# Attention scores by pairs of heads in one pass, with keys and queries laid out through HBM

## The chip, the cores and the metric

The kernel runs on one core of a Trainium2 chip, as one launch. The metric is the device time of that launch in microseconds (us).

## What is computed

The input x is (16, 96, 16, 16). The reference, cut to its parts:

```
x = conv_lstm(x)        # row by row recurrence over 16 rows, 48 features; skip conv; x + skip
t = tokens(x)           # (16, 256, 96): 256 tokens of 96 channels for each of 16 samples
q, k, v = six heads of 16 from layernorm(t)
scores = einsum('bhtd,bhsd->bhts', q, k) * 96 ** -0.5 ; causal mask ; softmax
t = t + (scores @ v, heads joined) @ Wp + bp
t = t + ffn(layernorm(t))   # 4 experts of 384 hidden, top 2 of 4, gelu
```

The weight and projection matmuls before the softmax and the router are done with operands split into a high and a low part (fp32r), so that three products make one of near float32 accuracy.

## The kernel before, in words

The kernel is written with one program for each engine, and semaphores between them. It has two stages. First comes the recurrence, which ends at about 81 us of the span. Then a loop over NBLK = 8 blocks of BT = 512 tokens, that is two samples (a = 0, 1) of two tiles (t = 0, 1) of 128 tokens. The first and the last block are written out, the rest is a loop.

Within a block the attention is done in NU = 10 units, listed in UNITS. A unit is some heads of one tile: for t = 0 (128 keys) HG[0] = 3 heads, so 384 columns of scores; for t = 1 (256 keys) HG[1] = 2 heads, so 512 columns. So units 0, 1 and 5, 6 have 384 columns, units 2 to 4 and 7 to 9 have 512. Scores go into one of two PSUM banks S[u % 2], probabilities into one of three slots of p_sb.

For each unit: TensorE makes the scores (L942 to L966) and adds the causal mask with a bf16 matmul (L965); VectorE takes the negated row maximum (L704); ScalarE the exponentials, an instruction per head, with their sum (L518); VectorE the reciprocal (L710); POOL scales the rows, an instruction per head (L406); TensorE transposes them (L976); VectorE or ScalarE copies the transposes (L457, which of them by PT_ON_ACT); TensorE multiplies with the values (L997). After the last unit of a tile ScalarE copies the heads' output (L527) and TensorE projects it (L1003), and VectorE makes the residual and its statistics (L717 to L721), from which POOL makes the reciprocal deviation (L389, L391).

The order on TensorE is written out by hand in its body (L1040). In step j it makes the scores of unit j + 2, then FILL[j] pieces of the expert output of the block before (L1018), then the values of unit j - 1, then the transposes of unit j. After the last step come the next block's queries and keys (L853 to L855), the transposes of the second layer norm (L1089), the hidden layer of the experts in 12 chunks of three matmuls (L1034, L1035, L1038), with the router between them. The scores of the next block's unit 0 stand after the ninth chunk (L1106), those of unit 1 after the last chunk and the values' projection (L1111). Block 0 has no expert output of a block before.

**Keys and queries.** ScalarE and VectorE split the projected queries into q_cur (high, low) and the keys into k_cur (high, low), 96 rows of 6 heads x 16 (L498, L691, L502, L696). Six heads are used as two triples. q_st holds for each triple 48 rows of high parts and 48 rows of low parts. k_bd holds block-diagonal keys: for each head of the triple its own columns, in pass 0 the high part against both halves of the query rows, in pass 1 the low part against the high queries. The rest of k_bd is zero, from a memset at the start (L375). So each group of scores takes two matmuls (L960, L962). The copies run on DMA from one place of SBUF to another, issued by SP (SyncE): per block 4 for the queries (load_queries, L289) and 24 for the keys (load_keys, L318: for each sample, triple and head one of 32 KB and one of 16 KB). In block 0 the query copies are issued by POOL (L441 to L443). SP's order in a block (body, L334): wait for the last scores of the block before, queries, wait for the low keys, keys of the first sample, store the output of an earlier block (L332), keys of the second sample, stage the tokens of a later block (L316). A wait that must stand alone on its instruction is made by wait_alone (L271).

TensorE waits for the queries and for the keys of the sample and triple that a unit needs (L945 to L953). At a block's end ScalarE waits for all the copies before it overwrites q_cur and k_cur (L551 to L555).

Of the kernel before, what the change touches and what calls it, by code (L numbers as in the profile page):

```python
# [20 lines left out]
F32 = mybir.dt.float32  # L21
# [13 lines left out]
HEADS, HS = 6, 16  # L35
# [14 lines left out]
HG = (3, 2)  # L50
UNITS = [(a, t, h) for a in range(2) for t in range(2) for h in range(0, HEADS, HG[t])]
NU = len(UNITS)
TILE_END = [1 + max(u for u, (a, t, _) in enumerate(UNITS) if 2 * a + t == s) for s in range(SPB)]
# [8 lines left out]
def hybrid_kernel(nc, x, w_input, w_state, b_skip, wq, wk, wv, wp, bp,  # L62
                  gate_w, gate_b, w1, b1, w2, b2, ident, ident_bf, causal_bf, lower, out):
    with ExitStack() as ctx:
# [183 lines left out]
        q_in = [sem("q_in0"), sem("q_in1")]  # L248
        q_in_first = [sem("q_in_first0"), sem("q_in_first1")]
        kbd_in = [[sem(f"kbd_in{a}{g}") for g in range(2)] for a in range(2)]  # L250
# [13 lines left out]
        KBD = 6 * 16  # L264
        TRI = 3 * HS
# [16 lines left out]
        def queries_taken(eng, n, g):  # L282

            if isinstance(n, int) and n == 0:
                eng.wait_ge(q_in_first[g], 32)
            else:
                eng.wait_ge(q_in[g], 32 * n)

        def load_queries(eng, g, taken):  # L289

            for part in range(2):
                eng.dma_start(as_f32(q_st[part * TRI:(part + 1) * TRI, g, :]),
                              as_f32(q_cur[g * TRI:(g + 1) * TRI, part, :])).then_inc(taken[g], 16)


        @block.sync
        def _(sp):
# [20 lines left out]
            def load_keys(a, g):  # L318

                cols = slice(a * 2 * TT, (a + 1) * 2 * TT)  # L320
                for i in range(3):
                    h = 3 * g + i
                    rows_h = slice(h * HS, (h + 1) * HS)
                    upper, lower_ = slice(i * HS, (i + 1) * HS), slice(TRI + i * HS, TRI + (i + 1) * HS)
                    sp.dma_start(as_f32(k_bd[upper, a, :, g, i, :]), as_f32(k_cur[rows_h, :, cols])
                                 ).then_inc(kbd_in[a][g], 16)
                    sp.dma_start(as_f32(k_bd[lower_, a, 0, g, i, :]), as_f32(k_cur[rows_h, 0, cols])
                                 ).then_inc(kbd_in[a][g], 16)
# [5 lines left out]
            def body(n, first=False, store=True, more=True):  # L334
                if first:
                    sp.wait_ge(klo_done, 1)
                    load_keys(0, 0)
                    load_keys(0, 1)
                else:
# [32 lines left out]
        def _(pool):  # L372
# [26 lines left out]
            def scale(n, u):  # L399

                wait_alone(pool, rden_done, NU * n + u + 1)
                _, t, _ = UNITS[u]
                nk = TT * (t + 1)
                for i in range(HG[t]):
# [44 lines left out]
        def take_pt(eng, n, u, first=False):  # L449

            t = UNITS[u][1]
            w = HG[t] * (t + 1) * TT
# [8 lines left out]
        def _(act):  # L461
# [48 lines left out]
            def exps(n, u, first=False):  # L510
# [4 lines left out]
                _, t, _ = UNITS[u]  # L515
                nk = TT * (t + 1)
                for i in range(HG[t]):
# [11 lines left out]
            def body(n, first=False, last=False):  # L529
# [19 lines left out]
                if not last:  # L549

                    for per_sample in kbd_in:  # L551
                        for taken in per_sample:
                            act.wait_ge(taken, KBD * (n + 1))
                    for g in range(2):
                        queries_taken(act, n, g)  # L555
                    take_q(n + 1)
                    take_k(n + 1)
# [28 lines left out]
        def _(dve):  # L586
# [112 lines left out]
            def row_max(n, u):  # L699

                _, t, _ = UNITS[u]
                nk = TT * (t + 1)
                dve.wait_ge(scores_ready, NU * n + u + 1)
                V.tensor_reduce(nmax[:, u % 3, 0:HG[t]], S[u % 2][:, 0:HG[t] * nk].rearrange("p (h k) -> p h k", k=nk),  # L704
                                AX.X, ALU.max, negate=True).then_inc(max_done, 1)

            def recip(n, u):
                dve.wait_ge(exp_done, NU * n + u + 1)
                hg = HG[UNITS[u][1]]
# [138 lines left out]
        def _(pe):  # L848
# [93 lines left out]
            def scores(n, u):  # L942
                a, t, h0 = UNITS[u]
                nh, nk, s = HG[t], TT * (t + 1), 2 * a + t
                if u >= 2:  # L945
                    pe.wait_ge(exp_done, NU * n + u - 1)
                elif u == 0:
                    pe.wait_ge(qlo_done, n + 1)
                    pe.wait_ge(klo_done, n + 1)
                if u < 2:  # L950
                    queries_taken(pe, n, u)
                if t == 0:
                    pe.wait_ge(kbd_in[a][h0 // 3], KBD * (n + 1))  # L953
# [249 lines left out]
```

## Time and profile before

| what | us |
|---|---|
| median of 3 runs | 471.73 (471.09 to 473.12) |
| span of the profiled execution, first to last instruction | 469.8 |
| recurrence | about 81 |
| TensorE busy | 429.3 (91%) |
| VectorE busy | 269.8 (57%) |
| ScalarE busy | 263.7 (56%) |
| POOL busy | 146.5 (31%) |

The profile shows one execution. Its own time is given as its span; the median of the runs is 1.9 us above it. Busy TensorE matmuls overlap each other, so that the mean duration of one is longer than what it adds to the time; the chain of work that ended last, read in order of time, gives what each adds. "Idle before, releaser" tells how long an engine waited and for what. PEld is TensorE's load of the stationary operand, beside the matmuls. SPq is SP's queue of DMA issues. The granted clock of TensorE is 1.00 at 2.4 GHz and 0.50 at 1.2 GHz.

### The profile page before, as it was taken

Reading aid. Unit: us, or ns where it says so; the run is one execution under the profiler, and the core shown is the slowest. Engines: PE = TensorE matmul, PEld = TensorE weight load, DVE = VectorE, ACT = ScalarE, POOL = GpSimd, SP = SyncE. Lnnn points to the kernel's source line nnn. Section 1 sums busy time; section 2 is a strip of 40 time slices with the busy share of each in tenths; the row PEclk is TensorE's granted clock in tenths of the full one; section 3 lists DMA queues with packets and bytes.
Section 4 is the critical chain, followed back from the end, with each engine's and each line's share of the span. In section 5 each row is a group of like instructions: output and inputs, shape, how many; then the busy total and the mean of one; then the engine's idle time right before and its main releaser. Section 6 shows DMA issues by size and latency. Waiting matters only on the chain.

```text
span 469.8 us, 10623 instructions
## 1 busy us (share of the span) xinstructions
PE 429.3 (91%) x3112; PEld 344.1 (73%) x3112; DVE 269.8 (57%) x954; ACT 263.7 (56%) x740; POOL 146.5 (31%) x309
## 2 busy tenths in 40 slices
PE   6999995449779999999999999999999999999897
PEld 6989994325558767877787787778767877787676
DVE  3888887445523853585277527743763586267424
ACT  2444453236557556664866485568556664866370
POOL 5000000235521542254236215531543254235200
PEclk9999998557979999999999999999999999999999
DMA  8500000031021002100210121012002100210000
GB/s 201 130 0 0 0 0 0 17 71 32 3 57 29 19 0 59 44 17 14 66 38 0 38 51 28 0 46 52 19 0 54 46 0 4 76 22 3 7 11 17
DMA packets 14392, 14.93 MB, mean 32 GB/s; under 512 B 5426, under 2 KB 11412, under 8 KB 14372
## 3 DMA queue, kind: packets, MB, share of 16 engines
q1 hardware_dynamic: 14180, 14.30, 12.1%
q0 software_dynamic: 192, 0.39, 0.3%
q8 instruction: 9, 0.15, 0.1%
q14 instruction: 11, 0.09, 0.1%
HBM read 3.86 MB, written 1.57 MB: 12 GB/s over the span
## 4 chain that ended last, share of the span: by engine, by line
PE 73%; DVE 12%; ACT 5%; issue 5%; SPq 2%; DMA 1%; POOL 1%; DVEq 1%; ACTq 0%; POOLq 0%
PE F L1018 18%; PE T L976 9%; PE A L997 8%; PE F L1034 4%; PE F L1038 4%; PE S L960 4%; PE F L1035 4%; PE S L962 3%; PE F L1014 3%; PE S L965 2%; DVE c L629 2%; DVE ig L627 2%; ACT tc_sb L471 2%; DVE pt_sb L457 1%; PE M L939 1%
## 5 line engine op out<-in xcount | busy, mean ns | idle before, releaser
L406 POOL TENSOR_SCALAR p_sb<-p_sb,rden 128x128 f32<-128x128 f32 (+1 forms) x192 | 79.8, 431 | 135.0 <-DVE rden L710 132.8
L1018 PE MATMUL F<-w_sb,hid 128*128 128x96 f32 x768 | 101.0, 276 | 0.0
L1018 PEld LDWEIGHTS F<-w_sb,hid 128*128 128x128 f32 x768 | 93.4, 192 | 6.0 <-issue 6.0
L518 ACT ACTIVATE p_sb<-S,nmax 128x128 f32<-128x128 f32 (+1 forms) x192 | 78.9, 425 | 17.1 <-DVE nmax L704 17.0
L704 DVE TENSOR_REDUCE nmax<-S 128x2 f32<-128x512 f32 (+1 forms) x80 | 50.7, 634 | 52.7 <-PE S L965 52.3
L457 ACT COPY pt_sb<-T 128x512 f32<-128x512 f32 (+1 forms) x48 | 26.4, 550 | 68.7 <-PE T L976 68.7
L564 ACT ACTIVATE hid<-F,b_sb 128x512 f32<-128x512 f32 x72 | 49.3, 686 | 9.6 <-PE F L1038 9.0
L997 PE MATMUL A<-pt_sb,v_cur 128*32 128x128 f32 x576 | 44.2, 284 | 8.5 <-ACT pt_sb L457 4.5
L976 PE MATMUL T<-id_sb,p_sb 128*128 128x128 f32 x288 | 49.2, 290 | 1.5 <-POOL p_sb L406 1.4
L960 PE MATMUL S<-k_bd,q_st 96*128 96x384 f32 (+2 forms) x96 | 39.3, 416 | 6.5 <-DMA k_bd<-k_cur 6.4
L976 PEld LDWEIGHTS T<-id_sb,p_sb 128*128 128x128 f32 x288 | 30.9, 143 | 16.3 <-issue 13.9
L518 ACT ACTIVATION_READ_ACCUMULATOR p_sb<-S,nmax 128x1 f32 x192 | 39.9, 208 | 0.0
L997 PEld LDWEIGHTS A<-pt_sb,v_cur 128*32 128x32 f32 x576 | 22.3, 109 | 20.4 <-ACT pt_sb L457 9.5
L962 PE MATMUL S<-k_bd,q_st 96*128 96x384 f32 (+2 forms) x96 | 32.9, 349 | 0.0
L779 DVE SCALAR_TENSOR_TENSOR y_sb<-F,gw,y_sb 128x96 f32<-128x96 f32 x96 | 30.5, 318 | 3.4
L1034 PE MATMUL F<-x2hi,w1hi 96*128 96x512 f32 x72 | 30.6, 425 | 1.4 <-ACT x2hi L559 0.8
L865 PE MATMUL F<-x_pad,win_sb 96*112 (+1 forms) x192 | 27.2, 291 | 4.5 <-DMA x_pad<-in_x 4.5
L457 DVE COPY pt_sb<-T 128x384 f32<-128x384 f32 (+1 forms) x32 | 20.0, 624 | 18.4 <-PE T L976 18.4
L1038 PE MATMUL F<-x2lo,w1hi 96*128 96x512 f32 x72 | 29.7, 413 | 0.0
L471 ACT ACTIVATE tc_sb<-c 48x128 f32<-48x128 f32 x32 | 9.9, 309 | 35.2 <-DVE c L629 35.2
L1035 PE MATMUL F<-x2hi,w1lo 96*128 96x512 f32 x72 | 28.9, 401 | 0.0
L865 PEld LDWEIGHTS F<-x_pad,win_sb 96*112 96x112 f32 x192 | 24.9, 193 | 4.4 <-DVE win_sb L596 4.4
(140 smaller groups left out, 781.8 us busy)
## 6 DMA issues: line engine op xcount, KB each, us to landing
k_bd<-k_cur SPq DMA_DIRECT2D x96, 32.0 KB, 2.0
q_st<-q_cur SPq DMA_DIRECT2D x28, 96.0 KB, 2.2
k_bd<-k_cur SPq DMA_DIRECT2D x96, 16.0 KB, 1.8
t_st<-t_cm SPq DMA_DIRECT2D x7, 192.0 KB, 2.4
out_y<-y_sb SPq DMA_DIRECT2D x7, 192.0 KB, 1.9
x_pad<-in_x SPq DMA_DIRECT2D x2, 612.0 KB, 8.6
w_sb<-in_w SPq DMA_DIRECT2D x1, 576.0 KB
hid<-in_w SPq DMA_DIRECT2D x1, 576.0 KB, 6.9
```

Source lines behind the costliest of these rows:

```text
L406: last = nc.gpsimd.tensor_scalar(p, p, rden[:, u % 3, i:i + 1], 1.0, ALU.mult, ALU.mult)
L457: copy(pt_sb[:, u % 2, 0:w], T[:, 0:w]).then_inc(pt_done, 1)
L518: last = nc.scalar.activation(p_sb[:, u % 3, i * nk:(i + 1) * nk], S[u % 2][:, i * nk:(i + 1) * nk], ACT.Exp, bias=nmax[:, u % 3, i:i + 1] ...
L564: nc.scalar.activation(hid[:, c, :], L1[c % 4][:], ACT.Gelu, bias=b1_sb[:, c:c + 1]).then_inc(gelu_done, 1)
L704: V.tensor_reduce(nmax[:, u % 3, 0:HG[t]], S[u % 2][:, 0:HG[t] * nk].rearrange("p (h k) -> p h k", k=nk), AX.X, ALU.max, negate=True).then ...
L865: last = mm(G[q][0:GATE_M, c * HC:(c + 1) * HC], wi_sb[:, tap, c], xr[:, bs, tap:tap + W], start=(c == 0 and tap == 0), stop=ready, skip_g ...
L960: mm(d, q_st[:, g, ts], k_bd[:, a, 0, g, i0:i1, 0:nk], start=(3 * g + i0 == h0), stop=False, skip_group_check=True)
L976: last = nc.tensor.transpose(T[:, i * TT:(i + 1) * TT], p_sb[:, u % 3, i * TT:(i + 1) * TT], id_sb[:])
L997: last = mm(A[VW * (h % 3):VW * (h % 3) + VW, 0:TT], v, pt_sb[:, u % 2, c0:c0 + TT], start=(kt == 0 and h < 3), stop=(kt == t and h >= 3), ...
L1018: last = mm(dst[:, e * C:(e + 1) * C], hid[:, c, s * TT:(s + 1) * TT], w2_sb[:, c], start=False, stop=(c == NCH - 1), skip_group_check=True)
L1034: mm(dst, w1hi[:, cs], x2hi[:], start=True, stop=False)
L1038: mm(dst, w1hi[:, cs], x2lo[:], start=False, stop=True).then_inc(hid_ready, 1)
```

## The change

For t = 0 a unit is now 4 heads and then 2, in place of 3 and 3; for t = 1 it stays at 2. Heads are used in three pairs. q_st holds for each pair 96 rows: 32 rows of high, 32 of low, 32 of high parts. k_bd holds for each pair 96 rows, the high keys, the high keys and the low keys, block-diagonal for the two heads and for all 512 tokens. One matmul makes the scores of a pair.

The layout is made in HBM. Per block SP issues: q_cur stored to q_hbm (1), the key parts high, high, low stored to their places in k_hbm (3), then, once each has landed, the query rows loaded (3, one for each 32 rows of q_st) and the keys loaded (3, one for each pair): 10 in place of 28. k_hbm is laid out so that a store of 6 heads x 16 rows puts each head's rows into its own columns; its zeros are stored once, at the start, from the zeroed k_bd (2 transfers). In all blocks these transfers are SP's. Before the query store SP waits for the key and query loads of the block before. TensorE waits for all query rows and for a pair's keys, ScalarE as before for all.

The diff, cut to its core (the rest hands the number of heads nh of a unit through the helpers):

```diff
-HG = (3, 2)
-UNITS = [(a, t, h) for a in range(2) for t in range(2) for h in range(0, HEADS, HG[t])]
+HG = (4, 2)
+NPAIR = HEADS // 2
+PAIR = 2 * HS
+UNITS = [(a, t, h, min(HG[t], HEADS - h)) for a in range(2) for t in range(2) for h in range(0, HEADS, HG[t])]
...
-        q_st = sb("q_st", [C, 2, BT], F32R)
+        q_st = sb("q_st", [C, NPAIR, BT], F32R)
...
-        k_bd = sb("k_bd", [C, 2, 2, 2, 3, 2 * TT], F32R)
+        k_bd = sb("k_bd", [C, NPAIR, 2, BT], F32R)
+        q_hbm = nc.dram_tensor("q_hbm", [C, 2, BT], F32, kind="Internal").ap()
+        k_hbm = nc.dram_tensor("k_hbm", [2 * PAIR * NPAIR * 2 * BT + HEADS * (HS * NPAIR * 2 + 1) * BT], F32, kind="Internal").ap()
...
+        QIN, KBD = 3 * 16, 16
+        Q_PARTS, K_PARTS = (0, 1, 0), (0, 0, 1)
...
+        def pair_taken(eng, n, g):
+
+            eng.wait_ge(q_in, QIN * (n + 1))
+            eng.wait_ge(kbd_in[g], KBD * (n + 1))
...
+            KROW = NPAIR * 2 * BT
+            KHEAD = HS * KROW + BT
+            KROWS = C + (NPAIR - 1) * PAIR
+            k_rows = k_hbm[0:KROWS * KROW].rearrange("(p c) -> p c", c=KROW)
+
+            def send_queries():
+
+                sp.dma_start(q_hbm[:], as_f32(q_cur[:])).then_inc(q_out, 16)
+
+            def send_keys():
+
+                for j, part in enumerate(K_PARTS):
+                    at = j * PAIR * KROW
+                    dst = k_hbm[at:at + HEADS * KHEAD].rearrange("(h s) -> h s", h=HEADS)
+                    dst = dst[:, 0:HS * KROW].rearrange("h (r c) -> h r c", r=HS)[:, :, 0:BT]
+                    sp.dma_start(dst, as_f32(k_cur[:, part, :])).then_inc(kbd_out, 16)
+
+            def fetch_queries(n):
+
+                wait_alone(sp, q_out, 16 * n + 16)
+                for j, part in enumerate(Q_PARTS):
+                    sp.dma_start(as_f32(q_st[j * PAIR:(j + 1) * PAIR]),
+                                 q_hbm.rearrange("(g r) p t -> p r g t", g=NPAIR)[part]).then_inc(q_in, 16)
+
+            def fetch_keys(n):
+
+                wait_alone(sp, kbd_out, 3 * 16 * (n + 1))
+                for g in range(NPAIR):
+                    sp.dma_start(as_f32(k_bd[:, g].rearrange("p x t -> p (x t)")),
+                                 k_rows[g * PAIR:g * PAIR + C, g * 2 * BT:(g + 1) * 2 * BT]).then_inc(kbd_in[g], 16)
...
             def body(n, first=False, store=True, more=True):
-                if first:
-                    sp.wait_ge(klo_done, 1)
-                    load_keys(0, 0)
-                    load_keys(0, 1)
-                else:
+                wait_alone(sp, qlo_done, n + 1)
+                if not first:
+                    for g in range(NPAIR):
+                        wait_alone(sp, kbd_in[g], KBD * n)
+                    wait_alone(sp, q_in, QIN * n)
+                send_queries()
+                wait_alone(sp, klo_done, n + 1)
+                send_keys()
+                if not first:
                     wait_alone(sp, scores_ready, NU * n)
-                    wait_alone(sp, qlo_done, n + 1)
-                    load_queries(sp, 0, q_in)
-                    load_queries(sp, 1, q_in)
-                    wait_alone(sp, klo_done, n + 1)
-                    load_keys(0, 0)
-                    load_keys(0, 1)
+                fetch_queries(n)
+                fetch_keys(n)
                 if store:
                     store_y(n - 2)
-                load_keys(1, 0)
-                load_keys(1, 1)
                 if more:
                     wait_alone(sp, tt_ready, n + 2)
                     stage(n + 2)
 
             sp.wait_ge(zeroed, 5)
+            for r0, r1 in ((0, C), (C, KROWS)):
+                sp.dma_start(k_rows[r0:r1], as_f32(k_bd[0:r1 - r0].rearrange("p g x t -> p (g x t)"))
+                             ).then_inc(kbd_zero, 16)
+            sp.wait_ge(kbd_zero, 32)
...
-            pool.wait_ge(qlo_done, 1)
-            load_queries(nc.gpsimd, 0, q_in_first)
-            load_queries(nc.gpsimd, 1, q_in_first)
...
-                for g in range(h0 // 3, (h0 + nh - 1) // 3 + 1):
-                    i0, i1 = max(h0 - 3 * g, 0), min(h0 + nh - 3 * g, 3)
-                    d = dst[:, 3 * g + i0 - h0:3 * g + i1 - h0]
-
-                    mm(d, q_st[:, g, ts], k_bd[:, a, 0, g, i0:i1, 0:nk], start=(3 * g + i0 == h0), stop=False,
-                       skip_group_check=True)
-                    mm(d, q_st[:, g, ts], k_bd[:, a, 1, g, i0:i1, 0:nk], start=False, stop=False,
+                ks = slice(a * 2 * TT, a * 2 * TT + nk)
+                for i in range(0, nh, 2):
+                    g = (h0 + i) // 2
+                    if a == 0 and t == 0:
+                        pair_taken(pe, n, g)
+                    mm(dst[:, i:i + 2], q_st[:, g, ts], k_bd[:, g, :, ks], start=(i == 0), stop=False,
                        skip_group_check=True)
```

## Rows read from the trace of the kernel before

**Rows 1.** The page: span, and part 1, busy time of each engine.

```profile
span 469.8 us, 10623 instructions
PE 429.3 (91%) x3112; PEld 344.1 (73%) x3112; DVE 269.8 (57%) x954; ACT 263.7 (56%) x740; POOL 146.5 (31%) x309
```

**Rows 2.** The page, part 4: the chain that ended last, by engine.

```profile
PE 73%; DVE 12%; ACT 5%; issue 5%; SPq 2%; DMA 1%; POOL 1%; DVEq 1%; ACTq 0%; POOLq 0%
```

**Rows 3.** Windows, one period of the loop: busy us (instructions), clock, DMA share, GB/s.

```profile
191.44:235.66 44.22, 43.20 (x320) 33.95 (x320) 25.15 (x87) 28.21 (x81) 17.16 (x37) 1.00 0.12 32
```

**Rows 4.** The chain in order of time, three units' scores: start us, us, what.

```profile
238.51 0.26 PE S L960
238.77 0.23 PE S L962
239.00 0.13 PE S L965
...
240.88 0.12 PE S L960
...
241.36 0.12 PE S L965
...
247.77 0.20 PE S L960
247.98 0.17 PE S L962
248.15 0.18 PE S L965
```

**Rows 5.** Groups by line and form: busy us, mean ns | idle before.

```profile
L406 POOL TENSOR_SCALAR p_sb<-p_sb,rden 128x128 f32<-128x128 f32 x96 | 34.8, 380 | 97.6 <-DVE rden L710 96.8
L518 ACT ACTIVATE p_sb<-S,nmax 128x128 f32<-128x128 f32 x96 | 34.3, 376 | 7.8 <-DVE nmax L704 7.8
```

**Rows 6.** Timeline of POOL and TensorE around unit 5: start us, us.

```profile
251.24 1.10 POOL L406 TENSOR_SCALAR p_sb<-p_sb,rden 128x128 f32<-128x128 f32 x3
...
252.84 0.55 PE L976 MATMUL T<-id_sb,p_sb 128*128 128x128 f32 x3
```

**Rows 7.** Timeline of four engines, from a block's keys to the next block's scores.

```profile
265.28 2.42 SPq L292 DMA_DIRECT2D q_st<-q_cur  x4
...
265.96 0.68 DVE L696 TENSOR_TENSOR k_cur<-S,k_cur 96x512 fp32r<-96x512 f32 x1
...
267.88 0.66 SPq L325 DMA_DIRECT2D k_bd<-k_cur  x1
...
275.30 0.34 PE L960 MATMUL S<-k_bd,q_st 96*128 96x384 f32 x1
```

**Rows 8.** DMA issues: count, KB each, median us from issue to landing.

```profile
out_y<-y_sb SPq DMA_DIRECT2D x7, 192.0 KB, 1.9
...
win_sb<-in_w_input SPq DMA_DIRECT2D x1, 252.0 KB, 3.0
```

**Rows 9.** The page, part 3: queue, packets, MB, share of 16 engines' span.

```profile
q1 hardware_dynamic: 14180, 14.30, 12.1%
```

**Rows 10.** DMA of 462 to 470 (the last stores), and GB/s in 40 slices of 187 to 191.

```profile
q1 hardware_dynamic: 288, 0.20, 7.7%
...
GB/s 0 0 0 0 92 113 92 31 0 0 61 82 21 0 0 0 108 353 338 399 353 307 108 0 0 82 102 103 41 0 0 41 92 31 0 0 0 0 72 113
```

**Rows 11.** Timeline of VectorE and TensorE at the first block's scores.

```profile
93.34 0.69 DVE L691 SCALAR_TENSOR_TENSOR q_cur<-S,q_cur 96x512 fp32r<-96x512 f32 x1 [0.60 <-ACT q_cur L498]
...
99.20 0.66 PE L960 MATMUL S<-k_bd,q_st 96*128 96x384 f32 x1 [4.87 <-DMA k_bd<-k_cur]
...
102.02 0.66 PE L960 MATMUL S<-k_bd,q_st 96*128 96x384 f32 x1 [1.50 <-DMA k_bd<-k_cur]
```

**Rows 12.** Windows around block 0's end; the column after POOL is the granted clock.

```profile
126.00:131.00 5.00, 2.50 (x18) 1.44 (x16) 2.18 (x7) 2.01 (x4) 1.72 (x5) 0.99 0.00 0
131.00:135.00 4.00, 3.24 (x9) 2.37 (x10) 1.19 (x2) 2.40 (x3) 2.03 (x2) 0.50 0.41 111
135.00:137.00 2.00, 2.00 (x6) 1.53 (x5) 0.00 (x0) 0.84 (x2) 0.00 (x0) 0.50 0.19 41
```

More of the change, by code:

```diff
@@ L47 @@
 GATE_STEPS = 14
-HG = (3, 2)
-UNITS = [(a, t, h) for a in range(2) for t in range(2) for h in range(0, HEADS, HG[t])]
+HG = (4, 2)
+NPAIR = HEADS // 2
+PAIR = 2 * HS
+UNITS = [(a, t, h, min(HG[t], HEADS - h)) for a in range(2) for t in range(2) for h in range(0, HEADS, HG[t])]
 NU = len(UNITS)
-TILE_END = [1 + max(u for u, (a, t, _) in enumerate(UNITS) if 2 * a + t == s) for s in range(SPB)]
+TILE_END = [1 + max(u for u, (a, t, _, _) in enumerate(UNITS) if 2 * a + t == s) for s in range(SPB)]
 FILL = [16, 3, 3, 2, 3, 3, 2, 2, 2, 0]
@@ L247, in hybrid_kernel @@
         t_staged = sem("t_staged")
-        q_in = [sem("q_in0"), sem("q_in1")]
-        q_in_first = [sem("q_in_first0"), sem("q_in_first1")]
-        kbd_in = [[sem(f"kbd_in{a}{g}") for g in range(2)] for a in range(2)]
+        q_in = sem("q_in")
+        q_out = sem("q_out")
+        kbd_out = sem("kbd_out")
+        kbd_zero = sem("kbd_zero")
+        kbd_in = [sem(f"kbd_in{g}") for g in range(NPAIR)]
         y_out = sem("y_out")
@@ L280, in as_f32 @@
             return ap.bitcast(F32)
-        def queries_taken(eng, n, g):
-            if isinstance(n, int) and n == 0:
-                eng.wait_ge(q_in_first[g], 32)
-            else:
[L287 to L293, printed above, removed]
+        def pair_taken(eng, n, g):
+            eng.wait_ge(q_in, QIN * (n + 1))
+            eng.wait_ge(kbd_in[g], KBD * (n + 1))
         @block.sync
@@ L316, in stage @@
                 sp.dma_start(t_st[:], t_cm[:, bass.ds(n * BT, BT)]).then_inc(t_staged, 16)
[L318 to L328, printed above, removed]
+            KROW = NPAIR * 2 * BT
[20 more added lines that the diff above has]
+                                 k_rows[g * PAIR:g * PAIR + C, g * 2 * BT:(g + 1) * 2 * BT]).then_inc(kbd_in[g], 16)
             def store_y(n):
@@ L401, in scale @@
                 wait_alone(pool, rden_done, NU * n + u + 1)
-                _, t, _ = UNITS[u]
+                _, t, _, nh = UNITS[u]
                 nk = TT * (t + 1)
-                for i in range(HG[t]):
+                for i in range(nh):
                     p = p_sb[:, u % 3, i * nk:(i + 1) * nk]
@@ L449, in take_pt @@
         def take_pt(eng, n, u, first=False):
-            t = UNITS[u][1]
-            w = HG[t] * (t + 1) * TT
+            _, t, _, nh = UNITS[u]
+            w = nh * (t + 1) * TT
             eng.wait_ge(pt_ready, NU * n + u + 1)
@@ L514, in exps @@
                     act.wait_ge(pt_ready, NU * n + u - 2)
-                _, t, _ = UNITS[u]
+                _, t, _, nh = UNITS[u]
                 nk = TT * (t + 1)
-                for i in range(HG[t]):
+                for i in range(nh):
                     last = nc.scalar.activation(p_sb[:, u % 3, i * nk:(i + 1) * nk], S[u % 2][:, i * nk:(i + 1) * nk],
@@ L549, in body @@
                 if not last:
[L551 to L555, printed above, removed]
+                    for g in range(NPAIR):
+                        pair_taken(act, n, g)
                     take_q(n + 1)
@@ L973, in probs_t @@
                     pe.wait_ge(x2lo_done, n)
-                t = UNITS[u][1]
-                for i in range(HG[t] * (t + 1)):
+                _, t, _, nh = UNITS[u]
+                for i in range(nh * (t + 1)):
                     last = nc.tensor.transpose(T[:, i * TT:(i + 1) * TT], p_sb[:, u % 3, i * TT:(i + 1) * TT], id_sb[:])
@@ L979, in values @@
             def values(n, u, first=False):
-                a, t, h0 = UNITS[u]
+                a, t, h0, nh = UNITS[u]
                 s = 2 * a + t
@@ L991, in values @@
                 for kt in range(t + 1):
-                    for i in range(HG[t]):
+                    for i in range(nh):
                         h = h0 + i
```

20 lines of the change are left out of this document (5 added, 15 removed).

## The prediction

> **What bounds the kernel now.** The page comes first: TensorE is busy in 91% of the span and makes 73% of the chain that ended last [rows 1, 2]. Then one period of the loop over blocks by windows: 44.22 us, of which TensorE is busy 43.20 [rows 3]. The six whole periods look alike. So an instruction taken off TensorE counts, as long as nothing else then ends TensorE's wait. The profiled execution spans 469.8 us, 1.9 below the median of 471.7; the sum is made against the span and 1.9 is added.
>
> **Part 1: fewer score passes.** Before, a unit multiplies each triple of heads twice, by the high and by the low part of the keys; after, each pair once, with the same 96 rows (q high, q low, q high against k high, k high, k low). The group view gives 416 and 349 ns for these matmuls, but they overlap; what one adds is read from the chain in order of time. A unit with 512 columns costs 0.26 + 0.23 and 0.13 for the mask; 256 columns cost 0.12; a unit with 384 costs 0.20 + 0.17 and 0.18 for the mask [rows 4]. A block has four units of 384 and six of 512, which the chain puts at 5.82 us in all. After, six units of 512 take one pass and the mask (0.39 each), two units of four heads take two passes of 256 and a mask of 512 (about 0.50), two of two heads one pass of 256 and a mask of 256 (about 0.27): 3.88. So 1.94 us a block, 15.5 in eight. The number of transposes, value matmuls, exponentials and reductions per block stays, and so do their widths in sum.
>
> **Part 2: units of 3 + 3 heads become 4 + 2.** Columns in sum are the same, but the first unit of each pair is longer. POOL takes 0.36 us per further head to scale, ScalarE about 0.35 (start to start; 376 and 380 ns each in the rows) [rows 5]. Before, POOL ends the scaling of unit 5 at 252.34 and its transposes start at 252.84: 0.5 spare [rows 6]. After, POOL ends 0.36 later, while TensorE comes about 0.5 sooner, because the scores of units 6 and 7 between the two have shrunk (0.28 and 0.23). So it waits some 0.3 there, and I take 0.2 more for the same at unit 7, behind the wider copy of unit 5: 0.5 a block given back, 4 in all. Bounds: nothing, and 1.5, if POOL, VectorE and ScalarE set the pace of all middle units.
>
> **Part 3: keys and queries through HBM.** Before, the scores of the next block's unit 0 start at 275.30, 8.66 after VectorE ends k_cur (265.96 + 0.68) [rows 7]. That distance stays: between them lie the x2 transposes, nine hidden chunks and the router, none of them changed. In it 12 SP issues and a landing had to fit; the first leaves at 267.88, 0.18 after the last query transfer, so a wait on SP costs about 0.18 [rows 7]. Now the rows must go out, land, and be fetched.
> SP: the queries are ready at 265.2; four new waits (three on keys, one on queries, all long met) put the query store at 265.9, the first key store at 266.8, the third at 268.1. The store of 192 KB lands 1.9 after its issue [rows 8]; about 0.8 of this is packets, so the first byte takes some 0.9, the close 0.2.
> How fast a store moves depends on how many DMA engines share it. Every larger transfer of the trace has an outermost dimension of 16, 48, 96, 112 or 128 rows; the new key store is written as 6 heads x 16 rows. One small case bears on it: the queue shows 14,180 packets [rows 9]; the pieces of its 258 transfers, one for each run of bytes in a row, add up to 10,066, which leaves 4,114 closing packets, 14 fewer than 258 x 16. Just the load of b2, with two rows, would be 14 short if it ran on 2 engines. So I take six engines for the key stores. The Trainium skill says this as a rule ("DMA: Bandwidth & Descriptors", why a DMA increments its semaphore by 16): the engines are the largest number up to 16 that divides the outermost dimension of both sides, here 6. By that rule the sum below stands; if a store always had 16 engines, the first rival would.
> One engine moves 20 GB/s in the last stores (0.20 MB in 7.7% of 8 us x 16 engines) and 25 at the best (399 GB/s over 16) [rows 10]. Three stores of 196 KB over six engines are 98 KB each, 3.9 to 4.9 us. They start behind the query store's packets at 268.0 and have landed at 272.1 to 273.1; SP sends the first two key loads at 272.3 to 273.3 and 0.65 later. Their bytes start 0.9 later, and on the six engines only after the query loads queued there (37 KB, 1.5 to 1.9 us: 273.4 to 274.8). Two key loads of 24.6 KB per engine take 2.0 to 2.6. Unit 0 can start at 275.6 to 277.8, where it was due at 275.30: a wait of 0.3 to 2.5; I take 1.5, the middle. As a check on this, a load of 252 KB lands after 3.0 [rows 8]. It falls on six of the seven hand-overs: at the first, block 0 runs at the lower clock and leaves 11.3 us. 6 x 1.5 = 9.0.
> Unit 1 needs pair 2, 0.65 later, and is due 3.4 after unit 0: covered. VectorE's maxima and the gelus shift with TensorE and are not late by themselves.
>
> **Part 4: the start.** Before, unit 0 runs at 99.20 and unit 1 at 102.02, both waiting for keys [rows 11]. Now SP stores the queries at 94.1 (after q_cur ends, 93.34 + 0.69), then the keys; six engines end at 100.4 to 101.3, the first two key loads have landed at 105 to 106, unit 1 follows at 106 to 107. Against 102.02 that is 4 to 5 later, and block 0 has no expert work of the block before to fill the gap: + 4.7. The stores of zeros (2 MB) run while the recurrence does, which ends at 81: nothing. The memset of k_bd halves, hidden too, as are the four query transfers that leave POOL and the 18 issues fewer on SP.
>
> **The sum.** 469.8 - 15.5 + 4.0 + 9.0 + 4.7 = 472.0; with 1.9 it is 473.9, say 474: the matmuls saved are given back in waits.
>
> **Rivals.** Half a percent, 2.4 us, is about what a measurement here can tell from no change.
> *Stores on all engines (faster).* The same bytes over 16 engines: 37 KB each, 1.5 to 1.9. The stores have landed by 270.1, while SP is issuing query loads until 271.1; key loads leave at 271.3 and 272.0 and have landed at 274.5 to 275.1, before 275.30. No wait in the loop, and a start later by 2.5: 469.8 - 15.5 + 4 + 2.5 + 1.9 = 462.7. For it: every large row shows full spread. Against: the count of closing packets. 0.25.
> *Six engines, but short waits.* The best ends of part 3 (0.3 to 0.7 a block): 474 - 6 x 1.0 = 468. 0.12.
> *The attention chain sets the pace (slower).* Its place is the scaling of unit 5 and of units 7 and 8 on POOL, where the spare before is 0.5; from there on each 0.1 that TensorE comes sooner is a wait of 0.1. If 1.5 of the 1.94 go back, it is 474 + 8 = 482. For: VectorE, ScalarE and POOL work through these units nearly without a gap. Against: their work in sum is unchanged, and the early units have more than 1 us spare. 0.15.
> *The clock falls (slower).* After a gap of 2.5 in block 0 the stretch 131 to 135 ran at 0.50, where 126 to 131 had 0.99, and was not back before 137 [rows 12], over 6 us. If a wait of over 2 us at the hand-over did this, some 3.3 more per block: 474 + 20 = 494. Against: before such a wait TensorE would have been busy without a pause, which it was not there. 0.03.
> That the two passes don't become one can't be: the loop issues one matmul per pair.
>
> **How the numbers follow.** Forecast 0.45, with 470 to 478 as its own range. Faster by over 0.5% (below 469.4): the first rival, most of the second, a little of the forecast: 0.34. Slower (above 474.1): the two slow rivals and half of the forecast: 0.39. The rest 0.27. The range goes from a little below the first rival, whose own bounds are as wide, to the third: 460 to 482.
>
> **What would show it.** One group of score matmuls x96 where there were two, a mean between 256 and 512 columns; a period near 44.2. At the hand-over, TensorE's wait for k_bd from k_hbm: 1.5 us, six times; key stores landing 4 to 5 us after the last issue (on 16 engines: 2). A small wait for POOL's p_sb before the transposes of units 5 and 7. Unit 1 of block 0 at 106 to 107. The forecast is wrong if the stores land within 2.5 us, or if the period is under 43.3 or over 45.

## The result, and the profile after

The changed kernel is slower, and by far more than forecast: 549.65 us in the median against 471.09 us for the kernel before in the same comparison, a ratio of 1.152 with a 95% interval of 1.144 to 1.160. The ratio takes only executions within 1.5% of the fastest of their kernel, here those of 540.9 and 545.2 us, so it lies below the quotient of the medians, 1.167. The forecast was 474, the range 460 to 482. The five executions of the changed kernel lie between 540.9 us, at a mean granted clock of 0.88, and 578.5 us, at 0.81: the stretches of low clock described below are not equally long in each. The profiled one took 570.9 us, at 0.82; times inside an execution are from it.

The page after: span, part 1 (busy time of each engine), the clock line of part 2 (granted clock in tenths, in 40 slices of 14.2 us), q1 of part 3, the engines of part 4, and one group of part 5.

```profile
span 569.1 us, 10328 instructions
PE 479.9 (84%) x3001; PEld 385.0 (68%) x3016; DVE 269.7 (47%) x954; ACT 262.8 (46%) x740; POOL 140.8 (25%) x305
PEclk9999975585656995699569955996799689959999
q1 hardware_dynamic: 13620, 30.84, 19.5%
PE 49%; DMA 16%; DVE 15%; issue 6%; ACT 5%; POOL 3%; SPq 3%; another core or an unknown queue 2%; DVEq 1%; POOLq 0%; ACTq 0%
L973 PE MATMUL S<-k_bd,q_st 96*128 96x256 f32 (+1 forms) x96 | 45.9, 492 | 50.0 <-DMA k_bd<-k_hbm 48.6
```

The work did shrink: 3001 matmul records for 3112 [rows 1], one group of score matmuls x96. Yet TensorE is busy 50.6 us longer, which no added work explains, and DMA makes 16% of the chain that ended last, where it made 1% [rows 2]. The clock line is the new thing: before, the digits were low in block 0 only, up to the twelfth slice of 11.7 us, as the page before shows:

```profile
PEclk9999998557979999999999999999999999999999
```

After, it dips in every block. Windows of after: one period of the loop (from one copy of x2hi to the next), then stretches inside it, and two at the start. The columns are those of [rows 3]; the clock is the third number from the end.

```profile
261.26:319.30 58.04, 51.47 (x308) 40.54 (x308) 25.14 (x86) 28.11 (x81) 17.07 (x37) 0.79 0.19 54
262.00:269.50 7.50, 7.50 (x33) 5.68 (x34) 2.26 (x8) 6.42 (x10) 2.71 (x3) 1.00 0.56 163
269.50:275.70 6.20, 1.09 (x4) 0.39 (x3) 0.00 (x0) 1.15 (x2) 0.00 (x0) 0.68 0.79 212
275.70:282.00 6.30, 6.30 (x19) 5.25 (x20) 0.69 (x1) 2.84 (x4) 0.00 (x0) 0.50 0.10 31
282.00:290.00 8.00, 8.00 (x32) 6.49 (x31) 3.19 (x15) 3.20 (x15) 1.42 (x4) 0.50 0.00 0
298.00:319.30 21.30, 19.94 (x173) 15.63 (x171) 15.21 (x53) 11.06 (x41) 11.03 (x26) 1.00 0.03 8
87.50:107.50 20.00, 4.51 (x15) 3.46 (x15) 5.29 (x8) 3.53 (x5) 1.27 (x1) 0.50 0.42 119
128.00:152.00 24.00, 19.24 (x81) 12.86 (x81) 8.09 (x23) 8.99 (x20) 7.83 (x15) 0.51 0.17 44
```

Read them in order. Up to 269.5 TensorE works without a pause at full clock. From 269.5 to 275.7 it is almost idle while the DMA engines are busy. Then it works without a pause again, at a granted clock of 0.50 (1.2 GHz), and only by 298 is it back at 1.00. The records put the fall at 271.8 and the return at 295.6: 23.9 us. VectorE and ScalarE, whose own work per period is unchanged (25.14 and 28.11 for 25.15 and 28.21), only wait for TensorE there.

What the idle stretch waits for stands in the chain of that stretch in order of time (start us, us, what):

```profile
260.52 0.60 DVE k_cur L715
...
261.19 0.79 SPq L337
...
262.80 7.37 DMA k_hbm<-k_cur
...
270.23 0.32 SPq L350
...
270.60 4.90 DMA k_bd<-k_hbm
...
275.63 0.55 PE S L973
```

and in the timelines of SP's queue and of TensorE over the same stretch:

```profile
260.39 0.33 SPq L329 DMA_DIRECT2D q_hbm<-q_cur  x1
261.19 2.28 SPq L337 DMA_DIRECT2D k_hbm<-k_cur  x3
263.89 3.42 SPq L343 DMA_DIRECT2D q_st<-q_hbm  x3
270.23 1.26 SPq L350 DMA_DIRECT2D k_bd<-k_hbm  x3
...
274.05 0.58 PE L973 MATMUL S<-k_bd,q_st 96*128 96x256 f32 x1 [4.11 <-DMA k_bd<-k_hbm]
275.63 0.55 PE L973 MATMUL S<-k_bd,q_st 96*128 96x256 f32 x1 [1.00 <-DMA k_bd<-k_hbm]
```

VectorE ends k_cur at 261.1; the last of three stores has landed at 270.2, 9.1 later; the second key load, issued at 270.6, lands at 275.5. Unit 0, now four heads, waits for pair 0 and again for pair 1: 4.11 + 1.00.

The DMA of 262 to 268, in 40 slices of 0.15 us (busy share of 16 engines in tenths, and GB/s):

```profile
DMA  9693432504433332631533443434597994536982
GB/s 300 273 382 137 150 82 27 55 14 96 96 96 82 96 82 96 137 68 68 150 123 123 109 109 96 96 96 96 191 232 273 355 355 178 137 137 150 205 150 96
```

From 263.3 to 266.2, where little but key stores moves, most slices show a share of 0.3 to 0.4 and a rate of 82 to 96 GB/s: 0.38 would be six engines of 16, and each then moves about 15 GB/s. From 266.2 on, with query loads issued by then, the rate rises to 355.

**The balance.** The period is 58.04 for 44.22, 13.8 more. The waits make 5.1 of it. Experiment e1_once below has the same passes and units at 43.23 without the waits, so these make -1.0. What is left, 58.04 - 43.23 - 5.11 = 9.7, is put down to the clock; experiment e4_fill below supports that. The other periods take 54.5 to 58.2. Over the run: the seven stretches from the first copy of x2hi (146.35) to the last (541.87) take 395.5 us against 310.5, so 85.0 more; the first copy comes 14.3 later (146.35 for 132.09); after the last both take 27.2. 85.0 + 14.3 is the whole difference of the spans, 99.3. The loop's 85.0 in turn: passes and units give back 7.4 (303.1 in e1_once for 310.5). TensorE's waits for keys make 33.1: the 48.6 of the page's L973 group less 15.5 in block 0. The rest, some 59, is again put down to the clock. The execution of 540.9 us has no profile. An estimate from its mean granted clock, 0.883 over 539.1 us, is 126 us at half clock, where the profiled one has 205 and the kernel before 39, so the clock is a large part of the loss there too, but a smaller one.

### The profile page after: what moved, and what is told of

It reads as the page before. It is cut to its first block, busy times and chain, and to the rows that moved or that the text cites. A ratio compares the mean times of both kernels' runs of the same rounds, so it can differ in the third digit from the quotient of the medians.

```text
span 569.1 us, 10328 instructions
## 1 busy us (share of the span) xinstructions
PE 479.9 (84%) x3001; PEld 385.0 (68%) x3016; DVE 269.7 (47%) x954; ACT 262.8 (46%) x740; POOL 140.8 (25%) x305
## 3 DMA queue, kind: packets, MB, share of 16 engines
q1 hardware_dynamic: 13620, 30.84, 19.5%
## 4 chain that ended last, share of the span: by engine, by line
PE 49%; DMA 16%; DVE 15%; issue 6%; ACT 5%; POOL 3%; SPq 3%; another core or an unknown queue 2%; DVEq 1%; POOLq 0%; ACTq 0%
PE F L1029 15%; DMA k_hbm<-k_cur 9%; PE T L987 8%; PE A L1008 7%; DMA k_bd<-k_hbm 6%; PE S L973 3%; PE M L958 2%; POOL p_sb L431 2%; SPq L337 2%; PE F L1025 2%; DVE xh L701 2%; DVE c L648 2%; DVE ig L646 2%; ACT tc_sb L493 2%
## 5 line engine op out<-in xcount | busy, mean ns | idle before, releaser
L1029 PE MATMUL F<-w_sb,hid 128*128 128x96 f32 x768 | 125.9, 321 | 0.5
L1029 PEld LDWEIGHTS F<-w_sb,hid 128*128 128x128 f32 x768 | 117.9, 235 | 7.8 <-issue 7.6
L723 DVE TENSOR_REDUCE nmax<-S 128x2 f32<-128x512 f32 (+2 forms) x80 | 50.3, 629 | 141.0 <-PE S L976 71.0
L540 ACT ACTIVATE p_sb<-S,nmax 128x128 f32<-128x128 f32 (+1 forms) x192 | 79.0, 425 | 50.8 <-DVE nmax L723 50.6
L973 PE MATMUL S<-k_bd,q_st 96*128 96x256 f32 (+1 forms) x96 | 45.9, 492 | 50.0 <-DMA k_bd<-k_hbm 48.6
L1008 PE MATMUL A<-pt_sb,v_cur 128*32 128x128 f32 x576 | 50.9, 298 | 10.0 <-ACT pt_sb L479 4.5
L973 PEld LDWEIGHTS S<-k_bd,q_st 96*128 96x128 f32 x96 | 21.7, 233 | 55.4 <-issue 27.1
L987 PE MATMUL T<-id_sb,p_sb 128*128 128x128 f32 x288 | 52.8, 305 | 4.5 <-POOL p_sb L431 4.5
L1008 PEld LDWEIGHTS A<-pt_sb,v_cur 128*32 128x32 f32 x576 | 27.2, 114 | 23.9 <-ACT pt_sb L479 9.8
L583 ACT ACTIVATE hid<-A,b_sb 128x512 f32<-128x512 f32 x24 | 16.3, 679 | 48.3 <-PE A L1049 48.3
L479 DVE COPY pt_sb<-T 128x512 f32<-128x512 f32 x32 | 22.1, 692 | 26.5 <-PE T L987 26.5
```

What stands on the lines that cost most here:

```text
L479: copy(pt_sb[:, u % 2, 0:w], T[:, 0:w]).then_inc(pt_done, 1)
L540: last = nc.scalar.activation(p_sb[:, u % 3, i * nk:(i + 1) * nk], S[u % 2][:, i * nk:(i + 1) * nk], ACT.Exp, bias=nmax[:, u % 3, i:i + 1] ...
L583: nc.scalar.activation(hid[:, c, :], L1[c % 4][:], ACT.Gelu, bias=b1_sb[:, c:c + 1]).then_inc(gelu_done, 1)
L723: V.tensor_reduce(nmax[:, u % 3, 0:nh], S[u % 2][:, 0:nh * nk].rearrange("p (h k) -> p h k", k=nk), AX.X, ALU.max, negate=True).then_inc(m ...
L973: mm(dst[:, i:i + 2], q_st[:, g, ts], k_bd[:, g, :, ks], start=(i == 0), stop=False, skip_group_check=True)
L987: last = nc.tensor.transpose(T[:, i * TT:(i + 1) * TT], p_sb[:, u % 3, i * TT:(i + 1) * TT], id_sb[:])
```

## The experiments

Eleven kernels ran. The periods are from one copy of x2hi to the next.

**1. Are passes and units worth what was said? e1_once** takes the changed kernel's layout transfers away after block 0; later blocks use block 0's keys and queries, so that part of the computation is left out.

```diff
-                send_queries()
...
-                fetch_keys(n)
+                if first:
+                    wait_alone(sp, qlo_done, n + 1)
+                    send_queries()
+                    wait_alone(sp, klo_done, n + 1)
+                    send_keys()
+                    fetch_queries(n)
+                    fetch_keys(n)
```

> Keys and queries are laid out for block 0 alone; the later blocks use those of block 0 (their own are left out), so SP moves nothing for them and TensorE never waits for a load after the start. Theory A (the loss is the wait at the hand-over and the lower clock that follows it): the period falls to 42 to 43.5 us, below the 44.2 of before, the clock stays at 1.00 in the loop, and the whole takes 455 to 468 us, the start's delay included. Theory B (the longer first units of each tile pair and the attention chain are the loss): the period stays above 46 us and the time above 485.

Measured: 478.5 us (477.6 to 480.9), ratio 1.017 [1.011, 1.022]. Windows of e1_once, one period:

```profile
235.73:278.96 43.23, 41.70 (x310) 33.01 (x308) 25.20 (x86) 28.10 (x81) 17.09 (x37) 1.00 0.03 9
```

The period is 43.23 where after has 58.04: without the transfers both the wait and the low clock are gone from the loop. So the transfers are the whole loss there. The total missed the 455 to 468 expected because of the start: the first block keeps its transfers, waits 14.3 us for the first keys and has its first copy of x2hi at 147.12, for 132.09 before. The start alone costs more (15.0) than passes and units save in the loop (7.4).

**2. Six engines or sixteen? e2_spread** writes each key store as 96 even rows. The keys then don't fall on their block-diagonal places; bytes and transfers are the same.

```diff
-                    dst = k_hbm[at:at + HEADS * KHEAD].rearrange("(h s) -> h s", h=HEADS)
-                    dst = dst[:, 0:HS * KROW].rearrange("h (r c) -> h r c", r=HS)[:, :, 0:BT]
+                    dst = k_hbm[at:at + C * KROW].rearrange("(p c) -> p c", c=KROW)[:, j * BT:(j + 1) * BT]
```

> The three key stores write the same bytes as 96 even rows, not as 6 heads x 16 rows (the block-diagonal places are left out; the loads are as they were). Theory A, with six DMA engines as the reason of the late landing: the stores land some 3 us after the last issue, not 7.4, the wait for keys at the hand-over falls from 5.1 us to under 2, and the time falls to 465 to 500 us, more of the loop at clock 1.00. If it is the way through HBM itself that is slow: the stores land after 6 us or more and the time stays above 530.

Measured: 514.1 us (499.7 to 521.0; the profiled execution is the 499.7). The queue of e2_spread (packets, MB, share), its DMA issues (count, KB each, median us from issue to landing), and its chain at one hand-over:

```profile
q1 hardware_dynamic: 13860, 30.84, 22.7%
...
k_bd<-k_hbm SPq DMA_DIRECT2D x24, 384.0 KB, 5.9
k_hbm<-k_cur SPq DMA_DIRECT2D x24, 192.0 KB, 2.9
...
230.73 3.43 DMA k_hbm<-k_cur
234.58 5.89 DMA k_bd<-k_hbm
```

The last store's landing comes 3.4 us after its issue instead of 7.4, from nothing but the shape of the destination. That after's stores run on six engines is also borne out by the count of packets: the data are cut into the same pieces, yet the queue shows 13,860 packets in e2 and 13,620 in after. That is 240 more for 24 stores, ten each, which fits one closing packet for each engine and 16 engines instead of 6. But the loads now take 5.9, so that the first forecast rival's "no wait in the loop" doesn't come true. TensorE still waits up to 0.8 and then 1.2 to 1.4 at six hand-overs, and at five of them stretches of 3 to 17 us at half clock follow. The median missed the 465 to 500 that was expected.

**3. The units, and a wait by accident: e3_units** is the kernel before with 4 + 2 heads for t = 0.

```diff
-HG = (3, 2)
+HG = (4, 2)
...
+                for g in range(h0 // 3, (h0 + nh - 1) // 3 + 1):
+                    if u < 2:
+                        queries_taken(pe, n, g)
+                    if t == 0:
+                        pe.wait_ge(kbd_in[a][g], KBD * (n + 1))
```

> The kernel before with units of 4 + 2 heads in place of 3 + 3, the two score passes and the copies as before. Theory A: 0 to 0.5 us more per block from POOL's longer first unit, 471 to 476 us. Theory B: 480 us or more.

Measured: 519.8 us (509.0 to 524.7), ratio 1.107 [1.098, 1.116]. Neither of the two theories is behind this. It is a wait I had not counted: the kernel before keeps triples, so four heads need the second triple's keys too, 12 transfers instead of 6 before unit 0. In the trace unit 0 waits 1.5 to 1.6 us for them at six hand-overs, each time followed by 3.4 to 13.7 us at half clock, and these periods take 48.1 to 52.8. The experiment mixed two things; the next three part them.

**4. That wait alone: e6b_wait12.** The kernel before, all units and transfers unchanged, but unit 0 also waits for the second triple.

```diff
+                if u == 0:
+                    pe.wait_ge(kbd_in[0][1], KBD * (n + 1))
```

> The kernel before with one wait more: unit 0 waits for the keys of both triples (12 transfers, landed at about 277) where it waited for one (6). Nothing else differs. Theory A: a wait of 1.6 us at each hand-over, after which the clock falls to 0.50 for 3 to 14 us, a period of 48 us or more and a time of 500 to 525 us. If so short a wait does not lower the clock, the period is 45.8 and the time 480 to 484.

Measured: 500.6 us (496.7 to 505.0), ratio 1.059 [1.054, 1.065]. Timeline of TensorE at one hand-over, and windows of three periods:

```profile
241.60 0.41 PE L962 MATMUL S<-k_bd,q_st 96*128 96x384 f32 x1 [1.58 <-DMA k_bd<-k_cur]
...
231.33:277.39 46.06, 43.45 (x322) 33.87 (x320) 25.12 (x86) 28.17 (x80) 17.05 (x37) 1.00 0.12 30
277.39:324.99 47.60, 45.00 (x322) 35.03 (x320) 25.13 (x86) 28.17 (x80) 17.07 (x37) 0.96 0.11 29
420.11:476.02 55.91, 52.30 (x307) 41.33 (x306) 21.27 (x71) 26.27 (x76) 15.83 (x35) 0.79 0.08 21
```

The wait is the same 1.5 to 1.6 us in these three. In the first period the clock stays at 1.00, and the period is 1.84 longer than 44.22. In the second it falls for 3.4 us; in the third for 20.5 and again for 3.4, and that period is 9.85 longer than the first although it holds less work: it is the last one, with no projections for a further block (43.14 for 44.22 in the kernel before). At the six hand-overs of the profiled execution at which TensorE ran at full clock and waited (1.5 to 1.8 us), the clock fell at five. The profiled execution is the longest of the four, 505.0 us.

**5. The same wait, with its gap filled: e11_wait12_fill** adds to e6b seven matmuls of 512 columns whose results are thrown away, ahead of the wait.

```diff
+                    if not first:
+                        pe.wait_ge(qlo_done, n + 2)
+                        for _ in range(7):
+                            mm(S[0][:], w1hi[:, 0:128], x2hi[:], start=True, stop=True)
```

> The kernel before with unit 0 waiting for 12 key transfers, as in e6b_wait12 (500.6 us), and 7 matmuls of 512 columns (1.6 us) whose result is thrown away ahead of that wait in every block but the first. If the clock is what made the 1.6 us of waiting cost 4 to 5 us a block, the clock now stays at 1.00 in the loop, the period is 45.8 to 46.0 us and the time 480 to 486 us. If something else in the later start of unit 0 costs it (the maxima, the exponentials), the time stays at 495 or more.

Measured: 484.5 us (483.9 to 485.2), ratio 1.030 [1.028, 1.033]. Timeline and windows of e11:

```profile
188.19 1.80 PE L1111 MATMUL S<-x2hi,w1hi 96*128 96x512 f32 x7
189.96 0.41 PE L962 MATMUL S<-k_bd,q_st 96*128 96x384 f32 x1
...
225.74:271.77 46.03, 45.01 (x328) 35.20 (x327) 25.12 (x86) 28.16 (x80) 17.06 (x37) 1.00 0.12 30
```

This pair carries the verdict. Unit 0 starts as late as in e6b (10.3 us after the copy of x2hi in both) and no useful work was added, but the time is 16 us less (14 by the ratios to the kernel before), the executions lie within 1.4 us where e6b's spread over 8, and the granted clock stays at 1.00 through the loop. From first to last copy of x2hi e11 takes 321.8 us, 11.3 more than before: 1.8 at each of six hand-overs, and 0.3 at the first. e6b takes 343.0: 21.2 more, and its low stretches in the loop sum to 44.3 us, half of which is 22.2.

**6. The units alone: e7b_once42.** The kernel before with 4 + 2, its transfers made in block 0 alone (later blocks use block 0's keys, as in e1).

```diff
-HG = (3, 2)
+HG = (4, 2)
...
-                    load_keys(0, 0)
-                    load_keys(0, 1)
...
+                if first:
+                    load_keys(1, 0)
+                    load_keys(1, 1)
```

> The kernel before with units of 4 + 2 heads, two score passes, and keys and queries laid out for block 0 alone (the later blocks use those of block 0), so that no wait for them is in the loop. It gives the price of 4 + 2 heads without the wait: Theory A, a period of 44.2 to 44.7 us and 470 to 478 us in all; theory B, over 46 and 485.

Measured: 484.4 us (478.7 to 484.9), ratio 1.023 [1.017, 1.029]. Windows of one period:

```profile
232.98:277.72 44.74, 43.65 (x324) 35.05 (x324) 25.30 (x86) 28.11 (x80) 17.11 (x37) 1.00 0.03 9
```

44.74 is 0.52 above 44.22, so the units don't explain the loss. But these 0.52 are not what 4 + 2 costs in the changed kernel. TensorE is idle for 44.74 - 43.65 = 1.09 in the period, where it was 1.02 before [rows 3]; it is busy 0.45 longer, with 324 matmuls for 320. With keys in triples, four heads reach into the second triple and take four score matmuls instead of two; pairs don't do that. The changed kernel's own price is read from e1: idle for 43.23 - 41.70 = 1.53, which is 0.51 more than before, and busy 1.50 less, which is what the passes give. The total of e7b is above the 470 to 478 expected by its start: block 0 ran from 123 to 147 at a granted clock of 0.51, and the first copy of x2hi stands at 141.16 for 132.09.

**7. After's own wait filled: e4_fill** adds 22 such matmuls, 5.3 us, before the next block's unit 0 in the changed kernel.

> The changed kernel with 22 more matmuls of 512 columns (some 5.1 us) ahead of the next block's first scores in every block but the first, their result thrown away. They fill the wait for the keys and add work. Theory A, clock part: the clock stays at 1.00 after the hand-over, the period falls from 58 to 46 to 49 us, and the time to 485 to 505 us although TensorE does more. If the clock has no part in it, the period stays at 58 and the time at 540 to 580.

Measured: 518.5 us (514.3 to 523.4), ratio 1.100 [1.089, 1.111]. Timeline and windows of e4:

```profile
251.53 5.29 PE L1120 MATMUL S<-x2hi,w1hi 96*128 96x512 f32 x22
...
257.56 0.36 PE L973 MATMUL S<-k_bd,q_st 96*128 96x256 f32 x1 [0.62 <-DMA k_bd<-k_hbm]
...
243.02:292.25 49.23, 47.06 (x332) 37.15 (x330) 25.20 (x86) 28.09 (x81) 17.16 (x37) 1.00 0.23 64
```

As the clock theory has it, the clock is 1.00 in the loop and the period 8.8 shorter than after's, with TensorE kept from its real work no less long (5.3 and 0.6 us). e1's period with these two added is 43.23 + 5.29 + 0.62 = 49.14, and 49.23 is measured: with the clock at 1.00 nothing of the 9.7 is left. In the whole it is 31 us by the medians and 25 by the ratios. The period is just above the 46 to 49 expected, and the start kept its 14 us, so the total is above the 485 to 505 expected.

**8. Pairs without HBM: e5b_direct.** The changed kernel's units and passes, with transfers from one place of SBUF to another: 18 for the keys on SP, 9 for the queries on POOL.

```diff
+        def load_keys(eng, pairs, js):
+            for g in pairs:
+                for h in (2 * g, 2 * g + 1):
+                    for j in js:
+                        r = j * PAIR + (h % 2) * HS
+                        eng.dma_start(as_f32(k_bd[r:r + HS, g, h % 2, :]),
+                                      as_f32(k_cur[h * HS:(h + 1) * HS, K_PARTS[j], :])).then_inc(kbd_in[g], 16)
```

> The changed kernel's pairs, units and single pass, with the copies from SBUF to SBUF as before: keys in 18 transfers of 32 KB on SP (high parts as soon as they are split off), queries in 9 of 64 KB on POOL, in block 0 the third pair's keys on ScalarE's queue. Theory A: the twelve key transfers that unit 0 needs land some 1 us before it is due, there is no wait at the hand-over, the clock stays at 1.00 in the loop, the period is 43.2 us as with transfers in block 0 alone, and the whole 462 to 468 us, under the kernel before. If less work on TensorE lowers the clock by itself, or the chain of the 4 + 2 units is the loss, it stays above 475.

Measured: 471.55 us (469.5 to 473.1), ratio 1.000 [0.998, 1.002]. Windows of one period:

```profile
226.30:269.57 43.27, 41.65 (x308) 33.02 (x308) 25.23 (x86) 28.11 (x81) 21.73 (x47) 1.00 0.14 36
```

The loop holds what the change had to offer: 43.27, no wait and no low clock. The total missed the 462 to 468 expected. The loop saves 6.6 us; block 0 gives 5.0 back, since its 27 transfers come before a start that nothing covers (unit 0 at 102.1 for 99.2, first x2hi at 137.06 for 132.09).

**9. The start, and a version that is faster.** e8_start issues block 0's transfers from SP, POOL and ScalarE. e9_warm adds thrown-away matmuls in the waits of block 0: 11 and 4 before the first projections, 20 before unit 0, 9 before the x2 transposes. e10_before_warm has these same matmuls in the kernel before.

```diff
+            def warm(k):
+                for _ in range(k):
+                    mm(T[:], idb_sb[:], warm_sb[:], start=True, stop=True)
...
+            warm(WARM_KEYS)
             scores(0, 0)
```

> As the direct copies (a median of 471.6), with block 0's 27 transfers spread over three queues: SP takes the high keys, ScalarE's queue the low keys and the third pair's queries, POOL the first two pairs' queries. Theory A (the gain of 0.95 us a block was eaten by the start): unit 0 of block 0 runs at 99.5 to 101 instead of 102.1, block 0 ends 2 to 3 us sooner, and the whole takes 467 to 470 us, 0.3 to 0.9% under the kernel before. If the start is set by the lower clock of block 0 and not by the keys, it stays at 471 to 472.

> As e8_start, and where TensorE waits in block 0 (for the first layer norm, for the keys, for the last layer norm) it runs matmuls whose result is thrown away: 11, 4, 20 and 9 of 512 bf16 columns. Theory A: the clock is back at 1.00 before the first scores and stays there, block 0's own matmuls take half the time, 455 to 464 us. If the clock is not what makes block 0 slow, the added work is a loss of 1 to 4 us.

> The kernel before with the same matmuls thrown away in block 0's waits. Theory A: it gains too, 460 to 467 us, so that what is left between it and e9_warm is the period's 0.95 us a block.

| kernel | median (lowest to highest) | ratio to before |
|---|---|---|
| e8_start | 469.9 (466.7 to 473.2) | 0.999 [0.996, 1.002] |
| e9_warm | 464.3 (462.8 to 467.6) | 0.989 [0.985, 0.992] |
| e10_before_warm | 468.6 (467.6 to 470.4) | 0.996 [0.994, 0.998] |

Windows of e9 over its start and block 0:

```profile
84.00:97.50 13.50, 9.22 (x46) 4.68 (x44) 3.91 (x8) 2.04 (x4) 5.78 (x9) 1.00 0.33 77
97.50:111.00 13.50, 8.73 (x33) 4.96 (x33) 6.97 (x13) 6.98 (x25) 3.10 (x8) 0.51 0.05 11
111.00:132.00 21.00, 16.35 (x130) 10.46 (x128) 12.79 (x47) 11.25 (x40) 11.60 (x27) 0.99 0.04 12
```

e8 can't be told from the kernel before. e9 is 1.1% faster than it, and the fastest kernel of this study, but it missed its 455 to 464 by 0.3: the clock fell once more for the first scores (97.5 to 111), which was not expected. Its clock is low for 23.9 us in all where the kernel before has 40.6. The matmuls give the old kernel 1.9 us and the pairs 5.6, so of e9's 6.2 us some 4.3 come from the pairs once the start doesn't eat them. e10 missed its range, probably because less of block 0 had been slow to begin with in the kernel before: 37.5 us at half clock, where e8 has 44.4.

## Why the prediction was wrong, step by step

**The clock, the main failure.** The sum put the clock at nothing; by the balance above it is some 59 us of the 85 by which the loop grew. The prediction had the mechanism only as its last rival, at 0.03: a wait "of over 2 us at the hand-over", "some 3.3 more per block", and against it that "TensorE would have been busy without a pause". All three failed. A wait of 1.5 to 1.8 us was enough at five hand-overs of six in e6b, where TensorE had come to it busy and at full clock, so a busy past is no protection. The price was 9.7 in the period of after shown above, with 23.9 us at half clock, three times what I had read from one stretch of block 0 [rows 12]. That row showed how the clock fell after a gap of 2.5 us; I read it as an oddity of block 0 and should have given the rival the chance of the wait itself. The Trainium skill ("TensorE: Matmul & The Clock Gate", Part 1) says that the throttled clock is the default and that activity releases it; e11 against e6b and e4 against after agree, since matmuls whose results nobody reads keep the clock at 1.00. A range that held this rival would have reached 494, and still have missed. The wait was also there at the first hand-over (1.06 + 1.13 in after), which the prediction had left out.

**The wait, 1.5 forecast, 5.1 measured.** Six engines was the right reading of [rows 9]; e2 shows it by its 240 further packets and by the landing, 3.4 for 7.4 after the last issue. The terms built on it were too small. *The rate:* 20 to 25 GB/s for one engine [rows 10] came from other transfers; the stores moved 82 to 96 GB/s in all, about 15 for each of six. The last store landed 9.1 after VectorE ended k_cur; I had 5.5 to 6.5. *The neighbours:* the query loads were issued while the stores still ran; no run tells what that cost. *The loads:* I had two key loads arriving 3 or so after their issue; the second landed 4.9 after, and e2 shows 5.9 with the stores spread. The rule of k engines (the Trainium skill, "DMA: Bandwidth & Descriptors", why a DMA increments its semaphore by 16) therefore agreed with the trace and wasn't enough by itself: it gives the number of engines, not what each moves. The rival with stores on 16 engines was priced at 462.7 and would have been wrong too: e2, which is that case, took 514.

**The passes, 1.94 a block forecast, 1.50 measured** (43.20 - 41.70 of busy TensorE, before and e1). The direction is right, as is the single group x96; the sum over the chain's gaps [rows 4] was 0.44 too large. I have no run that says which of its terms.

**4 + 2, 0.5 forecast, 0.51 measured** (1.53 - 1.02 of idle TensorE, e1 and before). The small wait for POOL is where it was put, before the transposes of unit 5: 0.28 us in e1 and 0.29 in after, for 0.3. Timelines of TensorE in e1_once and in after:

```profile
265.14 0.66 PE L984 MATMUL T<-id_sb,p_sb 128*128 128x128 f32 x4 [0.28 <-POOL p_sb L426]
...
247.44 0.66 PE L987 MATMUL T<-id_sb,p_sb 128*128 128x128 f32 x4 [0.29 <-POOL p_sb L431]
```

The other 0.2 was put at unit 7 and isn't there. In its place stand gaps of 0.14 and 0.08 ahead of value matmuls, so that the whole agrees partly by luck. The rival in which the attention chain sets the pace needed 1.5 more a block; e1's 0.51 leaves no room for it.

**The start, 4.7 forecast, 14.3 measured.** Unit 0 started at 107.5 and unit 1 at 110.1 where 106 to 107 was forecast, 8.1 behind before's 102.02 for the same causes as above. Another 6 came later in block 0, which ran at 0.51 from 128 to 152, where the kernel before was low for 6.8 us there. A later start moved the waits of block 0, and the clock with them; the prediction counted only the delay.

**The tests set out beforehand** worked: "wrong if the period is under 43.3 or over 45", and it was 58. A small slip changed nothing: the parts of "slower" add up to 0.41, not 0.39.

## What to carry to other kernels

Where TensorE is busy without a pause, price a new wait together with the clock that may fall behind it: six waits of some 1.6 us cost 11 us by themselves in e6b, and the clock another 21 in its profiled execution, 14 by the ratios. If such a wait can't be removed, matmuls without a use can fill it (14 to 16 us won in e11, 25 to 31 in e4). A layout trip through HBM is a store, its landing and a load, one behind another, and fewer DMA issues don't pay for it where those issues were hidden. A first block that has no neighbour's work to hide behind is to be priced by itself: in e5b it ate most of what the loop had won.

## What the runs showed of the hardware that was not expected

- A gap of 1.5 to 1.8 us in a stream of matmuls that was otherwise almost unbroken was followed in e6b by a granted clock of 0.50 in five of six cases, for 3.4 us (three times), 10.2 and 20.5; in e3, with 1.5 to 1.6, in six of six. At e4's first hand-over, which has no fill, TensorE waited 1.42 and 1.24 us and the clock stayed at 1.00; after, with 1.06 and 1.13 there, fell to 0.50 for 20.5 us. What decides whether it falls, and for how long, no run here tells.
- The same program then scatters: 540.9 to 578.5 us in after, 496.7 to 505.0 in e6b, but 483.9 to 485.2 with the gap filled.
- The issue of a key store took SP 0.76 us and that of a query load 1.14 (2.28 and 3.42 for three), against 0.33 for the query store.
- Key loads of 384 KB landed sooner (4.9 to 5.1) where the stores before them were slow than where they were spread over all engines (5.9 in e2). Which resource they share is open.
